# Eight tiles of dispatch's logits computed in attention's head, attention and dispatch in one block, and four places for the tokens' exponentials

## The reference

```python
xn = _layernorm(x)
x = x + attention(xn, wq, wk, wv, wo) + soft_moe(xn, ...)

# attention: 16 heads of 16 features, 4 key/value heads, causal softmax over 2048 tokens
att = softmax(where(causal, -inf, einsum('bsgmd,btgd->bgmst', q, k) / 4))
ctx = einsum('bgmst,btgd->bsgmd', att, v) @ wo.T

# soft mixture of 16 experts with 64 slots each: 1024 slots
x = layernorm(xn, norm_g, norm_b); se = layernorm(slot_embeds, slot_g, slot_b) * scale
logits   = einsum('bnd,esd->bnes', x, se)          # 2048 tokens x 1024 slots a batch
dispatch = softmax(logits, axis=tokens)            # over the tokens, for each slot
combine  = softmax(logits, axis=slots)             # over the slots, for each token
slots    = einsum('bnd,bnes->besd', x, dispatch)
eout     = (gelu(slots @ Wg + bg) * (slots @ Wu + bu)) @ Wd + bd
return einsum('bns,bso->bno', combine, eout)
```

## Time and profile before

| | us |
|---|---|
| median of three runs | 2688.85 (2688.53 to 2691.77) |
| the profiled execution's own time | 2690.94 |
| its span, first to last instruction | 2689.2 |
| project | 0 to 160.5 |
| attention's head | 160.5 to 204 |
| attention's steps with maxima | 204 to 1714.5 |
| attention's tail | 1714.5 to 1757 |
| L0 and L1 of dispatch | 1757 to 1873 |
| rest of dispatch | 1873 to 2208.9 |
| experts | 2208.9 to 2380.7 |
| combine | 2380.7 to 2689.2 |

### The profile page before, as it was taken

How to read it: one execution, slowest core, us unless ns; L and a number is a source line. 1 busy time by engine, 2 the same in 40 slices (tenths; PEclk the granted TensorE clock), 3 DMA queues, 4 the chain that set the end, 5 groups by cost and what they waited for, 6 DMA issues and landing times. The chain is left out here.

```text
span 2689.2 us, 47797 instructions
## 1 busy us (share of the span) xinstructions
PE 2580.5 (96%) x16291; PEld 1541.4 (57%) x16291; DVE 2046.0 (76%) x4879; ACT 1728.3 (64%) x3510; POOL 429.8 (16%) x676
## 2 busy tenths in 40 slices
PE   7989999999999999999999999998989999999999
PEld 4444444444444444444444444367877888889999
DVE  8779989989999998998998898468475523356665
ACT  4577777778777777777777777867656651222221
POOL 6601111111111111111111111223130100100000
PEclk9968999999999999999999999999999999999999
DMA  7945423303312321330330000044333354545554
GB/s 255 309 116 64 54 34 45 45 11 42 45 21 30 45 33 17 45 45 6 45 45 6 8 8 29 9 174 173 125 130 145 102 187 141 172 155 194 194 192 150
DMA packets 175855, 245.10 MB, mean 91 GB/s; under 512 B 57205, under 2 KB 129017, under 8 KB 174105
## 3 DMA queue, kind: packets, MB, share of 16 engines
q1 hardware_dynamic: 160088, 227.73, 33.8%
q10 hardware_dynamic: 15552, 14.68, 1.8%
HBM read 156.21 MB, written 84.97 MB: 90 GB/s over the span
## 5 line engine op out<-in xcount | busy, mean ns | idle before, releaser
L809 ACT ACTIVATE att_pr<-att_ring 128x512 f32<-128x512 f32 (+3 forms) x2560 | 1174.3, 550 | 330.7 <-PE att_ring L890 323.8
L857 DVE TENSOR_REDUCE att_mx<-att_ring 128x1 f32<-128x512 f32 x1536 | 967.6, 680 | 75.5 <-PE att_ring L903 73.1
L903 PE MATMUL att_ring<-att_ks,att_qs 48*128 48x512 f32 (+3 forms) x1920 | 647.3, 422 | 16.3 <-ACT att_pr L809 6.8
L890 PE MATMUL att_ring<-att_qs,att_ks 64*128 64x512 f32 (+3 forms) x1920 | 576.3, 406 | 6.6 <-DVE att_mx L863 2.3
L890 PEld LDWEIGHTS att_ring<-att_qs,att_ks 64*128 64x128 f32 x1920 | 300.4, 186 | 401.8 <-DVE att_mx L857 145.2
L863 DVE CUSTOM_DVE_ANT_0 att_junk<-att_ring,w_causal 128x256 bf16<-128x256 f32 (+3 forms) x1024 | 466.1, 486 | 57.6 <-PE att_ring L903 31.2
L932 PE MATMUL att_acc<-att_pr,att_v 128*17 128x512 f32 (+3 forms) x3840 | 453.8, 544 | 2.7 <-ACT att_cT L820 1.5
L903 PEld LDWEIGHTS att_ring<-att_ks,att_qs 48*128 48x128 f32 x1920 | 307.1, 185 | 142.1 <-ACT att_pr L809 103.5
L760 POOL TENSOR_SCALAR_AFFINE_SELECT att_pr<-att_pr 128x512 f32<-128x512 f32 x256 | 162.5, 635 | 1031.4 <-ACT att_pr L809 1031.4
L903 PE MATMUL att_ring<-g_ks,g_qs 48*128 48x512 f32 (+3 forms) x640 | 227.7, 467 | 15.5 <-PEq L152 5.8
L1513 ACT CAST com_e1h<-com_tp 128x1024 fp32r<-128x1024 f32 x64 | 64.7, 1016 | 236.3 <-PE com_tp L1573 236.3
(11 more groups left out here) (170 smaller groups left out, 3271.1 us busy)
## 6 DMA issues: line engine op xcount, KB each, us to landing
slot_exps<-dis_e SPq DMA_DIRECT2D x64, 512.0 KB, 2.7
com_e<-slot_exps SPq DMA_DIRECT2D x64, 512.0 KB, 3.5
att_qs<-q_parts SPq DMA_DIRECT2D x72, 256.0 KB, 12.0
q_parts<-proj_part SPq DMA_DIRECT2D x32, 512.0 KB, 5.0
dis_y<-in_L_attn_x_dram SPq DMA_DIRECT2D x64, 256.0 KB, 2.8
att_ks<-k_parts SPq DMA_DIRECT2D x72, 128.0 KB, 12.7
y_cols<-proj_yT SPq DMA_DIRECT2D x16, 512.0 KB, 5.3
context<-att_cn SPq DMA_DIRECT2D x64, 128.0 KB, 2.0
```

Of the source, the lines that this page charges most:

```text
L809: nc.scalar.activation(pr[:, s % NPR, h, off:CH], spot(("s", s, h)), ACT.Exp, scale=float(HD) ** -0.5).then_inc(exp_done, 1)
L857: nc.vector.tensor_reduce(dst, spot(e), AX.X, ALU.max).then_inc(mb_used, 1)
L890: nc.tensor.matmul(spot(e), ks[g][r, kb * P:(kb + 1) * P], qs[g][r, c, hf * CH + off:(hf + 1) * CH], start=True, stop=True).then_inc(sT_re ...
L903: nc.tensor.matmul(spot(e), qs[g][r, c, q0:q0 + P], ks[g][r, j * CH:j * CH + wd], start=True, stop=True).then_inc(mb_ready, 1)
```

## The change

1. **Logits in the head.** Each of 16 steps from step -17 on gets a new event "l": half a tile of batch 0's logits (6 matmuls of 512 columns into a bank of the ring). ScalarE copies it to the tile that later holds attention's exponentials and stores it to DRAM (`first_logits`) from its own queue; for the first twelve it does a piece of the zeroing in between, which is now cut into pieces of 2048 columns (six of them ahead of the first "l"). GpSimd splits the two chunks that this needs before anything else.
2. **Reload in attention's last group.** SP loads the eight tiles back to the place where dispatch wants them. In the tail VectorE takes their row and column maxima, up to two operations a step.
3. **Dispatch** has 8 tiles in L0. The 32 tiles of token exponentials of L0 and L1 are spread over the 24 slots that are left (`exps_by`), with four places in `e1` instead of two for those; the last two places are also where the slots' tiles lie later.
4. **One block** holds attention and dispatch, so that no barrier stands between them. TensorE waits for each bank by itself (`bank_free`); ScalarE waits for the context's stores before it writes where they are read.
5. **Other order of transfers.** Groups 1 and 2 are loaded in program order at steps -2 and 10, not -6 and 6, after the twelfth store of logits has landed; the queries of all four groups lie in one tile, in which `project` also keeps its parts.

```diff
+NE = 8
+QW = CPB * HL * CH
...
-    FIRST_LOADS = {-6: 1, 6: 2, 46: 3}
+    FIRST_LOADS = {-2: 1, 10: 2, 46: 3}
+    NL = 2 * NE
+    L_FROM = -LEAD + 5
+    L_LATE = NL - GS
+    ZP = (QW + S) // S
...
+        early = [("l", s - L_FROM)] if 0 <= s - L_FROM < NL else []
...
-        out = [st[0], xs[0], st[1], xs[1]] + ev + [xs[2], st[2], st[3], xs[3]] + av
+        out = [st[0], xs[0], st[1], xs[1]] + ev + [xs[2], st[2], st[3], xs[3]] + early + av
...
+            for n in range(NEC):
+                sp.dma_start(cols["low"][:, n].bitcast(F32), scr["yT_in"][0, n]).then_inc(cols["in"][n], 16)
             for s in ALL_STEPS:
                 if s in FIRST_LOADS:
+                    sp.wait_ge(l_out, 16 * L_LATE)
                     load_first(FIRST_LOADS[s])
...
+                if s == STEPS - NU + AV_LAG:
...
+                    sp.wait_ge(pv_done, (NBG - 4 + -(-NE // 4)) * NU)
+                    for t in range(NE):
+                        sp.dma_start(lg[:, t, :], scr["first_logits"][t]).then_inc(l_in, 16)
...
+            for n in range(NEC):
+                pool.wait_ge(cols["in"][n], 16)
+                hi, lo = cols["high"][:, n], cols["low"][:, n]
+                nc.gpsimd.tensor_copy(hi, lo.bitcast(F32)).then_inc(l_split, 1)
...
+            for k in range(NRG * ZP):
+                zero_rows(k)
             for s in ALL_STEPS:
+                for e in program(s):
+                    if e[0] == "l":
+                        act.wait_ge(mb_ready, turn[e] + 1)
+                        nc.scalar.copy(half_tile(e[1]), spot(e)).then_inc(l_kept, 1)
+                        if e[1] < (NKV - 2) * NRG * ZP:
+                            zero_rows(NRG * ZP + e[1])
+                        t, h = divmod(e[1], 2)
+                        act.wait_ge(l_kept, e[1] + 1)
+                        act.dma_start(scr["first_logits"][t, :, h * 512:(h + 1) * 512],
+                                      half_tile(e[1])).then_inc(l_out if e[1] < L_LATE else l_late, 16)
+                if s == 0:
+                    act.wait_ge(l_out, 16 * L_LATE)
+                if s == NPR - 1:
+                    act.wait_ge(l_late, 16 * (NL - L_LATE))
...
                 if not maxes_of(s):
                     row_maxes(s - 1)
                     inverse_sums(s)
+                    next(side, None)
+                    if s % 2:
+                        next(side, None)
...
+                    elif e[0] == "l":
+                        t, h = divmod(e[1], 2)
+                        wait_bank(pe, e)
+                        pe.wait_ge(l_split, 2 * (t // TPC) + 2)
...
+                            nc.tensor.matmul(spot(e), hi, seTh[:, k, to], start=(k == 0), stop=False)
+                            nc.tensor.matmul(spot(e), hi, seTl[:, k, to], start=False, stop=False)
+                            last = nc.tensor.matmul(spot(e), lo, seTh[:, k, to], start=False, stop=(k == DK - 1))
+                        last.then_inc(mb_ready, 1)
...
-        e1 = a.sb("e1", [P, 2, NS])
+        e1 = a.sb("e1", [P, 4, NS])
...
+        first_tile = lambda b: 0 if b else NE
+        SLOTS = 2 * TPB - NE
+        exps_by = lambda b, t: min(-(-2 * TPB * (b * TPB + t + 1 - NE) // SLOTS), b * TPB + t)
+        WIDE = 2 * TPB
+        place = lambda n: n % 4 if n < WIDE else n % 2
...
-                        for t in range(TPB):
-                            act.wait_ge(lp_ready, b * TPB + t + 1)
+                    for t in range(first_tile(b), TPB):
+                        act.wait_ge(lp_ready, b * TPB + t + 1 - NE)
...
-                            if t > 0:
-                                token_exp(b, t - 1)
+                        token_exps(exps_by(b, t) if b < 2 else b * TPB + t)
...
+            block = both.enter_context(nc.Block())
+            before = attend(nc, block, w, scr, g0, cols, queries, first_logits)
...
+            with both:
+                dispatch(nc, block, w, io, scr, pre, cols, first_logits, before)
```

More of the change, by code:

```diff
@@ L642, in place @@
             spot[1] += need
-        return where, before, {e: m[-1] for e, m in mates.items()}
+        return where, before, {e: m[-1] for e, m in mates.items()}, held
     NEAR = 4
     fills = [e for s in ALL_STEPS for e in program(s) if e[0] != "a"]
-    where, before, last_mate = place(fills)
+    where, before, last_mate, held_last = place(fills)
     turn = {e: n for n, e in enumerate(e for e in fills if e[0] != "s")}
@@ L653, in attend @@
         passed = a.sem("passed")
-        qs = [g0["qs"]] + [a.sb(f"qs{g}", [P, CPB, HL * CH], F32R) for g in range(1, NKV)]
+        qs = [queries[:, g * QW:(g + 1) * QW].rearrange("p (c n) -> p c n", c=CPB) for g in range(NKV)]
         ks = [g0["ks"]] + [a.sb(f"ks{g}", [P, S], F32R) for g in range(1, NKV)]
@@ L942, in dispatch, with bank_free, stored @@
+        def bank_free(pe, bank):
+            if bank < NBANK:
+                wait_read(pe, held_last[bank])
+            else:
+                pe.wait_ge(cT_ready, NBG * CPB)
+        def stored(eng):
+            for c in range(CPB):
+                eng.wait_ge(c_out[c], 16 * NBG)
+        return bank_free, stored
+def dispatch(nc, block, w, io, scr, pre, cols, first_logits, before):
     HB = SB // 2
@@ L949, in dispatch @@
     half_of = lambda ph: 2 * ph[1] + ph[2]
+    bank_free, context_stored = before
     early = lambda b: range(AHEAD) if b + 1 < B else range(0)
@@ new lines, in _, with split, column_maxes @@
+        @block.gpsimd
+        def _(pool):
+            def split(n):
+                if n < B * CPB:
+                    q = n % RING
+                    wait_apart(pool, yT_in[q], 16 * ((n - NEC) // RING), passed)
+                    nc.gpsimd.tensor_copy(yTh[:, q], yTl[:, q].bitcast(F32)).then_inc(yT_high, 1)
+                    pool.wait_ge(yT_high, n - RING - NEC + 1)
+                    nc.gpsimd.tensor_tensor(yTl[:, q], yTl[:, q].bitcast(F32), yTh[:, q].bitcast(F32),
+                                            ALU.subtract).then_inc(yT_split, 1)
+            def column_maxes(b):
+                wait_apart(pool, cm_done, TPB * (b + 1), passed)
+                for hf in range(2):
+                    h = slice(hf * 512, (hf + 1) * 512)
+                    nc.gpsimd.partition_all_reduce(cm[:, b % 2, h], cm[:, b % 2, h], P, RMAX).then_inc(ca_ready, 1)
+            for b in range(B):
+                if b:
+                    column_maxes(b - 1)
+                for n in range(b * CPB if b else NEC, b * CPB + CPB):
+                    split(n + RING)
+            column_maxes(B - 1)
```

1054 lines of the change are left out of this document (550 added, 504 removed).

## The result

The changed kernel takes 2678.74 us, median of seven runs (2676.13 to 2682.41), the kernel before 2688.85 beside it (2686.45 to 2691.77): ratio 0.9963, 95% interval 0.9953 to 0.9974. A second comparison gave 0.9964 (0.9951 to 0.9977). That is 10.1 us gained where 24.9 were forecast, and outside the range of 2658 to 2676. The sign was right, the size less than half.

A forecast was written before the change was run, and what follows sets the result against it. Bounds differed by stage: DVE in attention's head, ScalarE in its tail, TensorE then ScalarE and DVE in dispatch's first logits. Dispatch saves 26.9 us, the head costs 2: 24.9 saved, 2664 us, range 2658 to 2676.

The forecast's parts named there:

- Steps 1, 2 and 3: Dispatch: eight logit tiles fewer saves 22.4 us, the barrier before it gone 3.5, no slow start of its matmuls 2.1.
- Step 4: Dispatch's first logits: token exponentials of 32 tiles fitted into 24 slots cost 1.15 us, or 9.1 if uncovered.
- Step 5, the head: Before attention's first step: added half tiles, copies, zeroing and splits cost 2 us in sum, from -2 to +11.
- One or two steps at the lower clock therefore hide: Attention's head: banks let TensorE be some 3.6 us ahead, so one or two slow-clock steps cost nothing.
- The gain of 1 at the full clock afterwards: Attention's first steps after 204: no longer short of matmuls at full clock, 1 us saved, bounds 0 and 2.
- The DMA issues ... lie beside that zeroing: Attention's head: ScalarE's store issues, 0.38 us each, overlap its zeroing; + 3 us taken for ScalarE's pace, upper bound 8.9.
- ScalarE's issues: Rival, attention's head: the issues do not hide, 8.9 us in place of 3, 2670 us; chance 15%.
- the phases of logits did not become ScalarE's: Rival, dispatch: ScalarE bounds the logit phases, its 8 exponentials cost 9.1 us instead of 1.15, 2672 us; chance 12%.
- the clock neither swung nor stayed low: Two rivals, attention's head: half the steps slow, + 15, 2677 us, 7%; or all slow, + 30.2, 2692 us, 6%.
- the first exponential at 206: Sign in the profile after: attention's first exponential at 206 (204.69 before); the prediction is wrong if after 215.
- The steady part of attention grows by over 3 us: Sign against the prediction, which expected attention's steady part to stay as long as before.
- the third rival: Attention's head: TensorE's clock stays low throughout, + 30.2 us, 2692 us, deciding once more than 13 of 16 steps are slow; 6%.

The follow-up runs named there:

- changed_again: The changed kernel run once more with nothing changed, for a second profile; 2680.98 us, ratio to the kernel before 0.9964 (0.9951 to 0.9977).

## Why the prediction was wrong

- **Steps 1, 2 and 3** (eight tiles, barrier, slow start): right. 22.4, and 5.57 for the 5.6 of the last two; the experiments put the barrier at 1.8, and the wait for the context's store and the slow start behind it at 3.6. The branch showed nothing of its own: TensorE is idle for 0.47 where 0.4 was forecast. There is some luck in step 3, since the clock can be gone before TensorE's pause, as in changed_again (1 us).
- **Step 4** (token exponentials): right, 1.13 for 1.15. What it left out is VectorE. With the maxima phase unchanged in work, the splits of GpSimd came to lie beside it: 2.8 us in the profiled execution, 0.8 to 3.3 over the others. The phase moves by itself too, from 99.34 to 101.28 in the kernel before. Over the nine profiles with this order of work its mean is 79.9, against 100.3 for the two before: 20.4 gained of the 21.25 forecast.
- **Step 5, the head: this is the step that failed,** in two places. The smaller is its sum, + 3 for ScalarE's pace: the head took 7.0 more. ScalarE's pace had 2.2 in it, what is put down to TensorE 2.8, and the late rise of the clock 2.1. "One or two steps at the lower clock therefore hide" was wrong: VectorE idles 3.6 us in four waits from 167 to 177, as the head has just begun and no maxima are in store. The gain of 1 at the full clock afterwards rested on a clock that would stay, and it fell again at 211.
- The larger place is what stood in that step of **the stores: "The DMA issues ... lie beside that zeroing".** I priced their issue, which is right, and not their landing, for which ScalarE waits at step 0 and again at step 3. The rows to see it by were there: the earlier trace rows has a DMA share of 0.98 from 195 to 200 and 0.97 from 210 to 215, the loads of one head group, and the change puts those loads behind the twelfth store and ahead of the landing of the last four. ScalarE waits 8.1 us, and attention's path grew by some 6 to 7 of them, where the prediction had nothing; no rival had it either.
- Clock: it rose as forecast, in all profiles of kernels with half tiles, and fell again at the head's end in all of them, which nothing had foretold. ScalarE's issues did not show, the phases of logits did not become ScalarE's, the clock neither swung nor stayed low: no rival came true. Of the signs named, the first exponential at 206 came out by chance (206.08, with the projection 5.6 us shorter); it should have been put as a distance from the head's start. "The steady part of attention grows by over 3 us" was the sign that told.

- A slip in the sums of the third rival: "more than 13 of the 16 steps" leaves out the 3.6 us of banks that the sum before it takes off. With them it is more than 14 (14 x 2.11 - 3.6 = 25.9, 15 x 2.11 - 3.6 = 28.1, against 26.9).

What is open: why the clock rises late in some executions and early in others (2 us), why it falls at the head's end, and the 1 to 5 us that come and go in attention.

## What to carry to other kernels

A store has three prices, its issue, its landing and whoever waits for the landing; ask of each added transfer what else is in the DMA queues between the two, above all where the change itself has moved a burst. Moving the burst is not enough: behind it on its queue stands an order of waits, and two steps later in the program were 12.7 us later in time (224.23, 236.89). And measure a stage from its own start, since a stage ahead of it can move by more than the effect.

## What the runs showed of the hardware

- A 256 KB store landed in 2.0 us alone and in 12.1 (median of four), 15.8 at most, among 2.5 MB of loads, with the DMA engines full for 20 us. The Trainium skill (DMA: Bandwidth & Descriptors, Queues, rings and completion order) says that each DMA engine takes its queues in turn, a packet at a time; the queues' shares of 73.9% and 24.5% in that stretch agree with queues served side by side, and no row here shows the turns.
- VectorE's maximum of two tiles in SBUF went from 1.21 us to 2.65 and 3.43 beside GpSimd's work, each ending 1.1 us after GpSimd's operation, its reduction of one tile stayed at 1.21 (row 1824.12), and its reads from PSUM in the head lost nothing. The Trainium skill (GPSIMD Engine Reference, 1. Specifications) names just this, contention where VectorE has two inputs in SBUF; the rows agree.
- TensorE's clock stayed at 2.4 GHz through a pause of 2.26 us and fell to 1.2 in one of 3.86. It also fell with no pause over 0.8 us ahead of it: in changed_again at attention's end, with TensorE busy for 3.1 of 5 us, and at the end of the head (granted 0.59 from 210 to 215).
